# A transformer block pair on one core: y normalised token-major inside attention, and out-projection, feed-forward and the next projections as one software-pipelined stage

## The reference

```python
    x = L0_attn_a_x
    x = x + _L0_attn_a_ref(_layernorm(x, axis=-1), L0_attn_a_W_attn, L0_attn_a_W_proj)
    x = x + _L0_ffn_ref(_layernorm(x, axis=-1), L0_ffn_w1, L0_ffn_b1, L0_ffn_w2, L0_ffn_b2)
    x = x + _L0_attn_b_ref(_layernorm(x, axis=-1), ...)
    x = x + _L0_ffn_ref(_layernorm(x, axis=-1), L0_ffn_w1, L0_ffn_b1, L0_ffn_w2, L0_ffn_b2)
    return x
...
        att = _softmax(att, axis=-1)                  # both attentions, causal
        att = att * decay_weight_matrix(T)            # attention a only
...
        y = o @ Wo + bo                               # attention b; a has no bias
        mu = jnp.mean(y, axis=-1, keepdims=True)
        var = jnp.var(y, axis=-1, keepdims=True)
        return (y - mu) * jax.lax.rsqrt(var + EPS) * gamma + beta
...
        h = jnp.einsum('bsd,hd->bsh', x, bw1) + b1    # bw1, bw2: alpha * sign(w)
        h = jax.nn.gelu(h, approximate=False)
        out = jnp.einsum('bsh,dh->bsd', h, bw2) + b2
```

## Time and profile before

| what | us |
|---|---|
| three runs | 3030.36, 3037.56, 3042.88 (median 3037.56) |
| the profiled execution | 3037.05, its span 3035.3 |
| the two attentions | 1067.50 and 1069.90 |
| out_a, ffn_a, qkv_b | 144.30, 153.90, 127.70 (together 425.9) |
| out_b, ffn_b | 154.10, 153.70 (together 307.8) |

### The profile page before, as it was taken

The page is one execution under the profiler, slowest core; times in us unless marked ns, Lnnn a source line. Parts: engine busy times, 40 slices in busy tenths (PEclk is TensorE's granted clock), DMA queues, the critical chain, the costliest instruction groups (busy, mean ns, idle before and its releaser), DMA issues. The chain is left out here.

```text
span 3035.3 us, 45097 instructions
## 1 busy us (share of the span) xinstructions
PE 2530.0 (83%) x14016; PEld 1465.7 (48%) x14016; DVE 1994.2 (66%) x4919; ACT 1551.7 (51%) x3394; POOL 922.8 (30%) x1108
## 2 busy tenths in 40 slices
PE   4847999999999999477975698989889898984498
PEld 3523545455454454356743354545445454533477
DVE  5555777777877775245654686768667686725755
ACT  1206676685776867114421065656556565660144
POOL 0025777777787778200001101011010110112100
PEclk8958999999999999778988599999999999997799
DMA  4992145052350500683269905052350513008632
GB/s 152 268 146 37 23 67 65 25 82 32 55 82 9 82 12 9 105 174 118 84 181 244 121 12 78 8 81 33 56 77 8 81 29 60 12 8 142 151 124 70
DMA packets 195001, 242.97 MB, mean 80 GB/s; under 512 B 25297, under 2 KB 119378, under 8 KB 194002
## 3 DMA queue, kind: packets, MB, share of 16 engines
q1 hardware_dynamic: 177874, 223.36, 39.2%
q10 hardware_dynamic: 16896, 16.78, 1.9%
HBM read 143.99 MB, written 95.03 MB: 79 GB/s over the span
## 5 line engine op out<-in xcount | busy, mean ns | idle before, releaser
L700 POOL TENSOR_TENSOR att_a_wd<-att_a_wt,decay 128x256 f32<-128x256 f32 (+3 forms) x896 | 754.4, 872 | 287.7 <-PE att_a_po L892 139.8
L739 ACT ACTIVATE att_b_wt<-att_b_ps 128x512 f32<-128x512 f32 (+3 forms) x1280 | 597.1, 538 | 443.2 <-PE att_b_ps L867 438.2
L776 DVE TENSOR_REDUCE att_a_mpart<-att_a_pm 128x1 f32<-128x512 f32 x768 | 509.6, 686 | 180.4 <-PE att_a_pm L841 178.4
L776 DVE TENSOR_REDUCE att_b_mpart<-att_b_pm 128x1 f32<-128x512 f32 x768 | 503.4, 686 | 172.3 <-PE att_b_pm L841 171.6
L739 ACT ACTIVATE att_a_wt<-att_a_ps 128x512 f32<-128x512 f32 (+3 forms) x896 | 437.0, 507 | 248.6 <-PE att_a_ps L870 170.7
L841 PE MATMUL att_a_pm<-att_a_kop,att_a_qop 128*128 128x512 f32 (+3 forms) x1280 | 511.0, 422 | 40.1 <-DMA att_a_qop<-att_a_qop 29.0
L867 PE MATMUL att_b_ps<-att_b_qop,att_b_kop 128*128 128x512 f32 (+3 forms) x1280 | 459.6, 389 | 93.9 <-DMA att_b_qop<-att_b_mrow 89.1
L841 PE MATMUL att_b_pm<-att_b_kop,att_b_qop 128*128 128x512 f32 (+3 forms) x1280 | 502.2, 412 | 28.4 <-DMA att_b_qop<-att_b_qop 27.9
L841 PEld LDWEIGHTS att_a_pm<-att_a_kop,att_a_qop 128*128 128x128 f32 x1280 | 239.2, 194 | 289.9 <-DVE att_a_mpart L776 117.4
L841 PEld LDWEIGHTS att_b_pm<-att_b_kop,att_b_qop 128*128 128x128 f32 x1280 | 249.7, 198 | 261.9 <-DVE att_b_mpart L776 107.8
L718 POOL TENSOR_SCALAR_AFFINE_SELECT att_b_wt<-att_b_wt 128x512 f32<-128x512 f32 x128 | 81.3, 635 | 963.1 <-ACT att_b_wt L739 963.1
(11 more groups left out here) (189 smaller groups left out, 2632.9 us busy)
## 6 DMA issues: line engine op xcount, KB each, us to landing
att_a_kop<-qk SPq DMA_DIRECT2D x128, 128.0 KB
att_a_qop<-qk SPq DMA_DIRECT2D x128, 128.0 KB
att_b_kop<-qk SPq DMA_DIRECT2D x128, 128.0 KB
att_b_qop<-qk SPq DMA_DIRECT2D x128, 128.0 KB
qk<-qkv_a_qk_hi SPq DMA_DIRECT2D x32, 256.0 KB, 4.9
qk<-qkv_a_qk_lo SPq DMA_DIRECT2D x32, 256.0 KB, 4.3
v<-qkv_a_vt SPq DMA_DIRECT2D x32, 256.0 KB, 4.0
att_a_va<-v SPq DMA_DIRECT2D x8, 1024.0 KB, 22.5
```

The source lines that it names most:

```text
L700: pool.tensor_tensor(wd[:, kq % 2, j, a:z], wt[:, kq % buffers, j, a:z], keep["decay"][:, u:u + z - a], ALU.mult).then_inc(w_decayed, 1)
L739: act.activation(wt[:, kq % buffers, j, a:CH], pe_[:, seen % EBANKS, 0:CH - a], ACT.Exp)\
L776: dve.tensor_reduce(mpart[:, c, piece, u:u + 1], pm[:, n % MBANKS, 0:w], AX.X, ALU.max, negate=True).then_inc(m_reduced, 1)
```

## The change

In attention, the finished chunk of `y` is turned by PE to token-major in `px` (YT, L896 of the new file), and DVE takes the reciprocal of the row sums (in a, after it adds the far sums) and multiplies (YN); what SP stores is normalised, token-major, without padding, in 64 columns a group of heads. The turn and the store of the far sums (FT, FC) go. The copy `y` has one buffer for two. `v` in DRAM has 17 (a: 16) columns for a head in place of 32.

`output_projection`, `feed_forward` and the second `projections` become one function, `dense`, run as "mid" after attention a (with the projections) and as "end" after attention b (without them). Nothing between them is stored and loaded again. All engines walk one list, `dense_plan`: Y turns y, P is the out-projection (8 matmuls of the code a chunk, two k-tiles), N the normalisation of its result, X its turn, H and O as before, B the turn back, R the residual and in mid the next normalisation, Z the turn of that, Q the q and k matmuls and V the v ones. Y, X and Z share the PSUM tile `pt`; H and Q share the two banks of `ph`; P, V and B share `pp`. Roots are taken by POOL as a power of a 128x4 tile.

```diff
-        vt = sb("vt", [P, 2, TB, H, STRIP], F32)
+        VW = HD + v_ones
+        vt = sb("vt", [P, 2, TB, H, VW], F32)
...
-        cost = PV_TIME if item[0] != "O" else 0.0
+        cost = PV_TIME if item[0] in ("PO", "PV", "YT") else 0.0
...
+            follow(number + 3, GH - 1, ("YT", c))
...
+def apart(plan):
+
+    out, held, row_held = [], [], False
+    for item in plan:
+        if item[0] == "YT" and row_held:
+            held = [item]
+        elif item[0] == "YT":
+            out += [item, ("YN", *item[1:])]
+        else:
+            out.append(item)
+        if item[0] in ("MT", "MC"):
+            row_held = item[0] == "MT"
+        if held and not row_held:
+            out += held + [("YN", *held[0][1:])]
+            held = []
+    return out + [x for y in held for x in (y, ("YN", *y[1:]))]
 
 
...
-                follow((8, 0.0, ("FE", c)), (11, 0.0, ("FM", c)), (14, 200.0, ("FT", c)), (17, 200.0, ("FC", c)))
+                follow((8, 0.0, ("FE", c)), (11, 0.0, ("FM", c)))
...
                         for j in range(GH):
                             sp.dma_start(qop[MROW:MROW + 1, mpar, j, c * CH:(c + 1) * CH].bitcast(F32),
                                          mrow[TB * j:TB * j + TB, c, :].bitcast(F32)).then_inc(m_in[c], 16)
-                    if item[0] == "FC":
-                        _, d, c = item
-                        sp.wait_ge(x_read, x_use(g + d, c, 1) + 2)
-                        sp.dma_start(far_g[g + d, c], frow[:, FARS.index(c), :]).then_inc(f_out[c], 16)
-                    if item[0] == "O":
+                    if item[0] == "YN":
                         c = item[1]
-                        sp.wait_ge(o_kept, NC * g + c + 2)
-                        sp.dma_start(y_g[g, c], y[:, c % 2, :]).then_inc(y_out[c % 2], 16)
+                        sp.wait_ge(y_ready, done(g, c))
...
-                        act.wait_ge(y_out[c % 2], 16 * (2 * g + c // 2 + 1))
-                        act.activation(y[:, c % 2, :], po[:, :], ACT.Copy).then_inc(o_kept, 1)
+                        if done(g, c) > 1:
+                            act.wait_ge(y_turned, done(g, c) - 1)
+                        act.activation(y[:, :], po[:, :], ACT.Copy).then_inc(o_kept, 1)
...
+                    if item[0] == "YN":
+                        c = item[1]
+                        strips = px[:, :].rearrange("p (t j e) -> p t j e", t=TB, j=GH)
+                        near_sums = strips[:, :, :, HD].rearrange("p t j -> p j t")
+                        dve.wait_ge(y_turned, done(g, c))
+                        if c in FARS:
+                            dve.wait_ge(f_total, len(FARS) * g + FARS.index(c) + 1)
+                            dve.tensor_tensor(sums[:, :, :], near_sums, ftotal[:, c, :, :], ALU.add).then_inc(y_summed, 1)
+                            dve.wait_ge(y_summed, len(FARS) * g + FARS.index(c) + 1)
+                            dve.reciprocal(inverse[:, :, :], sums[:, :, :]).then_inc(y_inverse, 1)
+                        else:
+                            dve.reciprocal(inverse[:, :, :], near_sums).then_inc(y_inverse, 1)
+                        dve.wait_ge(y_inverse, done(g, c))
+                        dve.wait_ge(y_out[c % 2], 16 * (2 * g + c // 2 + 1))
+                        scale = inverse[:, :, :].rearrange("p j t -> p t j").unsqueeze(3).to_broadcast([P, TB, GH, HD])
+                        dve.tensor_tensor(yn[:, c % 2, :, :].rearrange("p t (j e) -> p t j e", j=GH),
+                                          strips[:, :, :, 0:HD], scale, ALU.mult).then_inc(y_ready, 1)
 
             steps(dve, step)
...
+                    if item[0] == "YT":
+                        c = item[1]
+                        pe.wait_ge(o_kept, done(g, c) + 1)
+                        wait_x_read(X_BEFORE.get(("YT", g, c)))
+                        for t in range(TB):
+                            mm = pe.transpose(px[:, t * P:(t + 1) * P], y[:, t * P:(t + 1) * P], keep["ident"][:, :])
+                        mm.then_inc(y_turned, 1)
...
-                            mm = pe.matmul(po[STRIP * j:STRIP * (j + 1), a:z], va[:, par, kb, j, :],
+                            mm = pe.matmul(po[STRIP * j:STRIP * j + VW, a:z], va[:, par, kb, j, :],
...
+def dense_plan(qkv):
+    plan = [("Y", 0), ("P", 0), ("N", 0), ("X", 0)] + [("H", 0, h) for h in range(EARLY)]
+    for G in range(CHUNKS):
+        follows = G + 1 < CHUNKS
+        for h in range(HT):
+            if 1 <= h < HT - 2:
+                plan.append(("H", G, h + 2))
+            elif h >= HT - 2 and follows:
+                plan.append(("H", G + 1, h + 2 - HT))
+            plan.append(("O", G, h))
+            if h == 0 and follows:
+                plan.append(("Y", G + 1))
+            if h == 1 and follows:
+                plan.append(("P", G + 1))
+            if h == 2 and follows:
+                plan.append(("N", G + 1))
+            if qkv and G and h == 3:
+                plan.append(("Z", G - 1))
+            if qkv and G and h == 4:
+                plan += [("Q", G - 1, 0), ("Q", G - 1, 1)]
+            if qkv and G and h == 5:
+                plan += [("Q", G - 1, 2), ("Q", G - 1, 3)]
+            if h == 5 and follows:
+                plan.append(("X", G + 1))
+            if qkv and G and h == 6:
+                plan.append(("V", G - 1))
+        if follows:
+            plan.append(("H", G + 1, EARLY - 1))
+        plan += [("B", G), ("R", G)]
+    if qkv:
+        G = CHUNKS - 1
+        plan += [("Z", G)] + [("Q", G, m) for m in range(2 * KT)] + [("V", G)]
+    return plan
...
+        ROTATION = [item for item in PLAN if item[0] in "HQ"]
+        TURNS = [item for item in PLAN if item[0] in "YXZ"]
+        PAIRS_USED = [item for item in PLAN if item[0] in "PVB"]
+        BANK = {item: k % 2 for k, item in enumerate(ROTATION)}
+        BEFORE = dict(zip(ROTATION[2:], ROTATION))
+        BEFORE.update(zip(TURNS[1:], TURNS))
+        BEFORE.update(zip(PAIRS_USED[1:], PAIRS_USED))
...
+                pool.wait_ge(var_ready, n + 1)
+                pool.tensor_tensor(rs[:, :], var[:, :], power[:, :], ALU.pow).then_inc(rs_ready, 1)
...
+                if item[0] == "P":
+                    if G == 0:
+                        pe.wait_ge(w_in, N_W)
+                    pe.wait_ge(yt_ready, G + 1)
+                    wait_pair(item)
...
+                if item[0] == "H":
+                    h = item[2]
+                    if (G, h) == (0, 0):
+                        pe.wait_ge(signs_in, 32)
+                    if h == 0:
+                        pe.wait_ge(hi_ready, G + 1)
+                        pe.wait_ge(lo_ready, G + 1)
+                    wait_bank(item)
+                    n = 0
...
+                if item[0] == "Y":
+                    act.wait_ge(y_turned, G + 1)
+                    if G:
+                        act.wait_ge(projected, G)
+                    act.activation(yt[:, :, :], pt[:, :, :], ACT.Copy).then_inc(yt_ready, 1)
+                if item[0] == "N":
+                    shifts += 1
+                    act.wait_ge(shift_ready, shifts)
+                    if G:
+                        act.wait_ge(x_turned, G)
+                    for t in range(TB):
+                        s = act.activation(xn[:, t, :], x1[:, par, t, :], ACT.Identity,
+                                           bias=shift[:, t:t + 1], scale=rs[:, t:t + 1])
...
+                if item[0] == "R" and qkv:
+                    shifts += 1
+                    act.wait_ge(shift_ready, shifts)
+                    if G:
+                        act.wait_ge(x2_turned, G)
+                    for t in range(TB):
+                        s = act.activation(xn2[:, t, :], x2[:, par, t, :], ACT.Identity,
+                                           bias=shift[:, t:t + 1], scale=rs[:, t:t + 1])
+                    s.then_inc(xn2_ready, 1)
+                if item[0] == "Z":
+                    act.wait_ge(x2_turned, G + 1)
+                    if G:
+                        act.wait_ge(v_done, G)
...
+                halves_variance(dve, var[:, :], half).then_inc(var_ready, 1)
+                norms += 1
+                dve.wait_ge(rs_ready, norms)
...
+                if item[0] == "P":
+                    dve.wait_ge(projected, G + 1)
+                    dve.wait_ge(x_in[par], 16 * (G // 2 + 1))
+                    if norm:
+                        dve.tensor_tensor(z[:, :, :], pp[:, :, :], bo[:, :].unsqueeze(1).to_broadcast([P, TB, D]),
+                                          ALU.add).then_inc(p_read, 1)
+                        dve.wait_ge(p_read, G + 1)
+                        moments(z, xn_done)
+                        for t in range(TB):
+                            s = dve.scalar_tensor_tensor(out=z[:, t, :], in0=z[:, t, :], scalar=mean[:, t:t + 1],
+                                                         in1=gamma[:, :], op0=ALU.subtract, op1=ALU.mult)
+                        s.then_inc(zg_ready, 1)
```

(33 more changed lines are left out.)

786 lines of the change are left out of this document (326 added, 460 removed).

## The result

The changed kernel took 3091.91 us (median of 4 runs, 3086.94 to 3094.90), the kernel before 3035.86 on the same chips: ratio 1.0182, 95% interval 1.0156 to 1.0208. It is slower by 1.8%. The forecast was 3092 us. That the two agree so closely is partly luck: of the terms, one was 17 us too low, one of 9 was missing on the other side, and the rest were within 5, both of them a little too high.

The account below looks back on a forecast made before the run. Attention was taken as PE-bound, mid and end as PE work plus waits and their clock loss. Span 3035.3 + 2 (mid) + 22 (end) + 31 (attention) + 1.75 around it = 3092 us; own range 3050 to 3125.

Parts of the forecast that it names:

- The walk: One chunk of mid followed step by step: 33.0 us of PE work plus 11.3 of waits, period 44.3 at full clock.
- the clock: Mid and end: matmuls behind a long wait run at half clock at first, 2.4 us lost each, 4.8 a chunk.
- The two long waits: Mid: PE waits 4.5 us before the out-projection P and 3.5 before the q and k matmuls Q.
- the third wait: Mid: 2.5 us between turn X and the next hidden matmuls; no clock loss charged, 1.9 a chunk kept for the range.
- the root: Layernorm chains of mid and end: POOL's power taken at 0.2 us, at 0.75 about 10 more in all.
- waits 1 and 2: Mid: before P, 4.5 us, from ACT's queue; before Q, 3.5, with the copy behind the second normalisation.
- the narrower v: Attention: v half as wide saves 2 us of loading at each stage's start, -4 in all.
- The waits did not stay short: Rival for mid and end: the two long waits are 1.5 to 2 us; 120 less, 2972 us; chance 0.15.
- the clock did not stay up: Rival for mid and end: no 4.8 a chunk lost behind waits; 3029 us, no measurable change; chance 0.10.
- PE was not the bound: Rival: PE bounds mid and end, at 33.0 and 21.2 us a chunk; 2870 us; chance 0.05.
- attention did not pay 32 more: Rival: DVE's maxima queue keeps YN late, delaying turned maxima, 64 x 0.5 us more; 3124 us; chance 0.12.
- the fast rival: Mid and end: waits stay short because DVE gets to the moments sooner, ACT and DVE having room; 2972 us; chance 0.15.

Follow-up runs that it names:

- run 1: Changed kernel, but in mid ACT copies the turned y and does the next gelu before normalising the chunk before: 3039.29 us, 1.0007 to the kernel before.
- run 2: Changed kernel, but turn X stands ahead of the second q and k pair in mid and the eighth hidden tile in end: 3042.46 us.
- run 9: Changed kernel, turned y copied before normalisation, X earlier, and in mid ACT's copy for q and k ahead of the next chunk's normalisation: 2961.38 us, 0.9753.
- run 5: Changed kernel with added matmuls of unused result in PE's waits (10, 8, 5 in mid; 10, 10, 5 in end): 3042.14 us, 1.0023 to the kernel before.
- Run 8: Changed kernel with v stored and loaded in strips of 32 columns again: 3107.36 us, 1.0228 to the kernel before.
- run 7: Changed kernel with the four turns of y done twice in each of the 64 attention chunk steps: 3121.65 us, 1.0276 to the kernel before.
- run 6: Changed kernel, but attention's turns of y are kept four items behind the copy of the turned maxima: 3074.94 us, 1.0128 to the kernel before.

## Why the prediction was right

- **Right, and shown: the waits of mid come from the order.** The walk gave 4.5, 3.5, 2.5 and 0.8; the trace has 4.89, 3.78, 2.42 and 0.63. That the first is ACT's queue is shown by run 1, that the third is the missing work behind X by run 2, that the second is an order too by run 9 (with the other two). The terms written down for the second add to 23.3 and not to 22.9, which makes its wait 3.9; the rows have 3.78.
- **Right in kind, mis-sized: the clock.** The term was 4.8 a chunk. From the period, 51.2 less 33.0 of work and 11.7 of waits, it is 6.5 in mid; run 5 gives 6.3. The two long waits cost 2.2 and 2.5 for the 2.4 of the forecast. What failed is the step on the third wait, "I charge nothing for it": behind it the rows show 1.6 lost, near the 1.9 that was kept only for the range. The period was thus 51.2 for 49.1, which is 12 of the 17 us that mid was too low; the other 5 lie in the first and the last chunks. In end the clock is 3.9 by the same reckoning and at least 2.3 by run 5, for 4.8 forecast; there nothing is lost behind the third wait, so that for end the step was right. The Trainium skill ("TensorE: Matmul & The Clock Gate", section "HAM oscillation — how this bites in real kernels") describes bursts of matmuls that each start cold behind a wait for DMA. The trace agrees for the long waits, which here are for ACT and DVE: the mean clock is 0.81 and 0.79 of full, and 0.92 and 0.95 once the waits are filled.
- **Mis-sized: the root.** Taken as 0.2 "since its 4 columns are far nearer to that"; POOL took 1.01 and DVE waited 1.12. The upper bound of the range, 755 ns, was itself too low: a row of additions bounds no power. The chain grew by 0.64, more than the 0.39 and 0.28 by which waits 1 and 2 exceed the walk.
- **Missing: v's store.** The prediction counted the narrower v at the two loads, -4 in all, and nothing in qkv_a, whose window shrank by 8.8. Run 8 gives 6.1 of them back and 11 in attention b. The 8.8 offset half of mid's miss, which is most of the luck in the total.
- **Right in sum, not by stage: attention.** +28.3 for +31, but 1081.7 and 1084.0 us where about 1095 and 1075 were forecast: 13 too high in a and 9 too low in b. The waits of the turns lie mostly in b (16.9 of 25.4). In the sum, the turns cost 28.8 (run 7) for 33; waits for the maxima's copy 25.4, of which 17 show (run 6), for 14; PE's waits for the copy of y 8.0 for 11; the wait for the rows of maxima -21.8 for -17, but half of that for another reason than the one given (run 8), and the other half not tested.
- **Right: end.** 325.4 for 329, with waits of 4.67, 4.71 and 2.42 for 4.7, 4.9 and 2.5, and a period of 37.6 for 39.
- **The rivals.** The waits did not stay short, the clock did not stay up, PE was not the bound, and attention did not pay 32 more. Run 9 shows that the fast rival's premise was sound, only not its order: in mid ACT and DVE do have the room.
